# Search for the 512th score: one of three levels a round summed as signs on ScalarE, its row work cut into pieces between the rounds

## The reference, cut to what matters

```python
scores = xf @ gate_w.T
scores = (jnp.tanh(scores) + 1.0) * 0.5
vals, idx = jax.lax.top_k(scores.T, k)          # k = 4096 // 8 = 512, n = 8 experts
kept_w = vals.T
flat_idx = idx.T.reshape(-1)
y = xf[flat_idx].reshape(k, n, d)
y = _layernorm(y, ln_gamma, ln_beta)
h = jnp.einsum('knd,nfd->knf', y, fc1s) + b1s
h = jax.nn.gelu(h, approximate=True)
o = jnp.einsum('knf,ndf->knd', h, fc2s) + b2s
o = o * kept_w[:, :, None]
out = xf.at[flat_idx].add(o.reshape(k * n, d))
```

## Time and profile before

| | before |
|---|---|
| median of 3 runs | 853.91 us |
| lowest and highest | 852.01 and 854.15 us |
| the profiled execution's own time | 856.66 us |
| its span, from the first to the last instruction | 854.9 us |
| TensorE busy | 663.0 us, 78% of the span |
| VectorE busy | 555.0 us, 65% |
| ScalarE busy | 432.2 us, 51% |
| GpSimd busy | 405.3 us, 47% |
| mean granted TensorE clock | 0.896 of full speed |

### The profile page before, as it was taken

The page is one execution under the profiler, slowest core; times in us unless marked ns, Lnnn a source line. Parts: engine busy times, 40 slices in busy tenths (PEclk is TensorE's granted clock), DMA queues, the critical chain, the costliest instruction groups (busy, mean ns, idle before and its releaser), DMA issues. The chain is left out here.

```text
span 854.9 us, 18149 instructions
## 1 busy us (share of the span) xinstructions
PE 663.0 (78%) x6567; PEld 417.3 (49%) x6567; DVE 555.0 (65%) x1594; ACT 432.2 (51%) x627; POOL 405.3 (47%) x583
## 2 busy tenths in 40 slices
PE   6748999999869999999977669999896413888500
PEld 3423555555435666666644336766664103555400
DVE  6977888888468898888887643544456884222116
ACT  5433777777745555555526656766662600232102
POOL 7853777777640000000016756665564502788743
PEclk9975999999979999999989978999997755899765
DMA  4774463431000000000004999999991340355354
GB/s 159 244 221 94 135 169 97 120 95 54 4 1 1 1 1 2 1 1 1 2 0 177 264 257 174 189 178 173 187 183 55 91 114 17 74 129 98 34 94 124
DMA packets 134839, 85.76 MB, mean 100 GB/s; under 512 B 11104, under 2 KB 131424, under 8 KB 134624
## 3 DMA queue, kind: packets, MB, share of 16 engines
q1 hardware_dynamic: 127968, 79.30, 40.7%
q0 software_dynamic: 5632, 4.33, 3.7%
q10 hardware_dynamic: 1152, 0.98, 0.4%
HBM read 54.70 MB, written 29.49 MB: 98 GB/s over the span
## 5 line engine op out<-in xcount | busy, mean ns | idle before, releaser
L2120 ACT ACTIVATE a_prob<-a_ps_pair 128x1024 f32<-128x1024 f32 x96 | 93.8, 1023 | 51.9 <-PE a_ps_pair L1956 34.0
L1791 ACT ACTIVATE a_prob<-a_ps_pair 128x1024 f32<-128x1024 f32 x96 | 96.5, 1023 | 14.0 <-PE a_ps_pair L1594 10.9
L2132 POOL TENSOR_SCALAR_AFFINE_SELECT a_prob<-a_prob 128x512 f32<-128x512 f32 (+1 forms) x96 | 76.8, 805 | 55.0 <-ACT a_prob L2120 54.8
L1832 POOL TENSOR_SCALAR_AFFINE_SELECT a_prob<-a_prob 128x512 f32<-128x512 f32 (+1 forms) x96 | 75.4, 787 | 42.0 <-ACT a_prob L1791 41.3
L1730 DVE TENSOR_REDUCE a_mx<-a_ps_pair 128x4 f32<-128x1024 f32 x64 | 77.8, 1221 | 24.5 <-PE a_ps_pair L1635 22.8
L922 POOL TENSOR_SCALAR xn<-xn,stats,norm_b_rstd 128x128 f32<-128x128 f32 x8 | 6.4, 805 | 175.0 <-POOLq L411 175.0
L478 PEld LDWEIGHTS m_ps_n<-wd,m_act 128*128 128x128 f32 x512 | 66.4, 192 | 29.0 <-issue 27.4
L701 ACT ACTIVATE m_up<-m_ps_u,m_bup 128x512 f32<-128x512 f32 x64 | 44.0, 687 | 65.4 <-PE m_ps_u L466 65.3
L590 DVE SCALAR_TENSOR_TENSOR xn<-m_ps_n,m_wt,xn 128x128 f32<-128x128 f32 x256 | 71.7, 343 | 0.2 <-DVE xn L590 0.2
L478 PE MATMUL m_ps_n<-wd,m_act 128*128 128x128 f32 x512 | 67.6, 275 | 1.0 <-DVE xn L590 0.8
L466 PE MATMUL m_ps_u<-m_x1T,wgu 128*128 128x512 f32 x128 | 67.0, 606 | 0.0
(11 more groups left out here) (287 smaller groups left out, 1525.8 us busy)
## 6 DMA issues: line engine op xcount, KB each, us to landing
qst<-scratch_q SPq DMA_DIRECT2D x64, 128.0 KB, 4.2
kst<-scratch_k SPq DMA_DIRECT2D x64, 128.0 KB, 4.2
scratch_q<-p_parts SPq DMA_DIRECT2D x16, 384.0 KB, 3.1
scratch_k<-p_parts SPq DMA_DIRECT2D x16, 384.0 KB, 2.8
qst<-scratch_q SPq DMA_DIRECT2D x32, 192.0 KB, 6.1
kst<-scratch_k SPq DMA_DIRECT2D x32, 192.0 KB, 6.0
...
```

The costliest lines, as they stand in the source:

```text
L1791: nc.scalar.activation(prob[:, r % 6, :], pair[(0, 2, 1)[j]][:, :], ACT.Exp, scale=scale, bias=0.0).then_inc(s_e, 1)
L1832: nc.gpsimd.affine_select(out=blk, in_=blk, compare_op=ALU.is_ge, fill=0.0, base=0, pattern=[[0, n], [1, P]], channel_multiplier=-1).then_ ...
L2120: nc.scalar.activation(prob[:, r % 6, :], pair[r % 2][:, :], ACT.Square, scale=scale, bias=1.0).then_inc(s_e, 1)
L2132: nc.gpsimd.affine_select(out=blk, in_=blk, compare_op=ALU.is_ge, fill=0.0, base=0, pattern=[[0, n], [1, P]], channel_multiplier=-1).then_ ...
```

## The change

Rounds 1 to 12 still test three levels, but VectorE counts only two of them. The third is done by ScalarE: it computes the sign of score minus level for all 256 columns and writes the sum of the signs into the third column of `count`. The sum of signs over 4096 scores is twice the count minus 4096, so the third flag compares with 2*512 - 4096 - 0.5 (`sides`). ScalarE adds its bias, so the third level is kept with a negative sign, and the steps have signs too. TensorE waits for both engines' columns. Round 13 tests two levels on VectorE, with four small operations after it in place of two. ScalarE's other work in the block is spread over the rounds: two tiles of `yn` after the signs of each of rounds 1 to 8, and a quarter of `twice` (two instructions of four tiles) after those of rounds 9 to 12. `yn` is therefore complete before `twice`, and SP stores it first; the store of `twice` gets a semaphore of its own, which GpSimd waits for ahead of the first scatter and not ahead of the gathers. One more constant is loaded. The diff, whole:

```diff
--- before.py
+++ after.py
@@ -972,8 +972,8 @@
 
 
     ident, F = consts["ident"], F1
-    wgp, table, same, lower, slot, row, own, sel4, tilew, gb = [consts["later"][n] for n in (
-        "wgp", "table", "same", "lower", "slot", "row", "own", "sel4", "tilew", "gb1")]
+    wgp, table, sides, same, lower, slot, row, own, sel4, tilew, gb = [consts["later"][n] for n in (
+        "wgp", "table", "sides", "same", "lower", "slot", "row", "own", "sel4", "tilew", "gb1")]
     NT = NTILE
     sum_d = nc.dram_tensor("sum", [NTOK, C], F32, kind="Internal").ap()
     rows_d = nc.dram_tensor("normed", [NTOK, ROW], F32, kind="Internal").ap()
@@ -997,8 +997,9 @@
         yn = sb("yn", [P, NT, ROW])
         tanh = sb("tanh", [P, T])
         score = sb("score", [P, T])
-        hit = sb("hit", [P, 3, T], BF16)
-        count, parted = sb("count", [P, 3], BF16), sb("parted", [P, 2], BF16)
+        hit = sb("hit", [P, 2, T], BF16)
+        side = sb("side", [P, T], BF16)
+        count, parted = sb("count", [P, 4], BF16), sb("parted", [P, 2], BF16)
         level, base = sb("level", [P, 4]), sb("base", [P, 4])
         flag = sb("flag", [P, 3])
         reached, thr, need, before_sel = [sb(n, [P, 1]) for n in ("reached", "thr", "need", "before_sel")]
@@ -1048,8 +1049,11 @@
         s_ynp = sem("rows_normalised_by_pool")
         s_w = [sem(f"expert_weights_loaded{i}") for i in range(2)]
         s_d = sem("rows_stored")
+        s_sd = sem("sums_stored")
         s_st = sem("vector_step")
+        s_level = sem("levels_ready")
         s_cnt = sem("rows_counted")
+        s_side = sem("sides_summed")
         s_tot = sem("tokens_counted")
         s_part = sem("flags_counted")
         s_pre = sem("prefixes_ready")
@@ -1096,12 +1100,12 @@
             def _(sp):
                 for e in range(2):
                     sp.dma_start(w[:, e, :], io["w1"][e, :, :]).then_inc(s_w[e], 16)
-                sp.wait_ge(s_two, 1)
-                sp.dma_start(sum_d.rearrange("(t p) c -> p t c", p=P), twice[:, :, :]).then_inc(s_d, 16)
                 sp.wait_ge(s_yn, NT // 2)
                 sp.wait_ge(s_ynp, NT // 2)
                 sp.wait_ge(s_scol, 2)
                 sp.dma_start(rows_d.rearrange("(t p) c -> p t c", p=P), yn[:, :, :]).then_inc(s_d, 16)
+                sp.wait_ge(s_two, 8)
+                sp.dma_start(sum_d.rearrange("(t p) c -> p t c", p=P), twice[:, :, :]).then_inc(s_sd, 16)
                 for e in range(2, E):
                     sp.wait_ge(s_ob, e - 1)
                     sp.dma_start(w[:, e % 2, :], io["w1"][e, :, :]).then_inc(s_w[e % 2], 16)
@@ -1148,8 +1152,9 @@
                 last.then_inc(s_stp, 1)
 
                 for r in range(ROUNDS):
-                    n = 3 if r + 1 < ROUNDS else 1
-                    pe.wait_ge(s_cnt, 3 * r + n)
+                    n = 3 if r + 1 < ROUNDS else 2
+                    pe.wait_ge(s_cnt, 2 * r + 2)
+                    pe.wait_ge(s_side, min(r + 1, ROUNDS - 1))
                     nc.tensor.matmul(ps_c[:, 0:n], same[:, :].bitcast(BF16), count[:, 0:n], start=True, stop=True).then_inc(s_tot, 1)
 
                 pe.wait_ge(s_part, 2)
@@ -1225,8 +1230,7 @@
                     ins.then_inc(s_st, 1)
                     ve.wait_ge(s_st, done[0])
 
-                v.tensor_copy(level[:, :], table[:, 0:4]).then_inc(s_st, 1)
-                done[0] += 1
+                v.tensor_copy(level[:, :], table[:, 0:4]).then_inc(s_level, 1)
                 for c in range(NCH):
                     if c == 4:
                         norm.invert_rest(ve, s_rest)
@@ -1242,25 +1246,29 @@
                 v.tensor_scalar(score[:, :], tanh[:, :], 1.0, 0.5, ALU.add, ALU.mult).then_inc(s_score, 1)
                 ve.wait_ge(s_score, 1)
                 for r in range(ROUNDS):
-
-                    step_size = table[:, 4 * r:4 * r + 1]
-                    for j in range(3 if r + 1 < ROUNDS else 1):
+                    steps = table[:, 8 * r + 4:8 * r + 8]
+                    ve.wait_ge(s_level, r + 1)
+                    for j in range(2):
                         v.tensor_scalar(hit[:, j, :], score[:, :], level[:, j:j + 1], 0.0, ALU.is_ge, ALU.add,
                                         accum_out=count[:, j:j + 1]).then_inc(s_cnt, 1)
                     if r + 2 < ROUNDS:
-                        v.tensor_scalar(base[:, :], table[:, 4 * r + 4:4 * r + 8], level[:, 3:4], None, ALU.add).then_inc(s_st, 1)
+                        v.scalar_tensor_tensor(base[:, :], sides[:, 0:4], level[:, 3:4], table[:, 8 * r + 8:8 * r + 12], ALU.mult, ALU.add)\
+                            .then_inc(s_st, 1)
                         done[0] += 1
                     ve.wait_ge(s_tot, r + 1)
+                    if r + 1 < ROUNDS:
+                        step(v.scalar_tensor_tensor(flag[:, :], ps_c[:, 0:3], 0.0, sides[:, 4:7], ALU.add, ALU.is_ge, accum_out=reached[:, :]))
                     if r + 2 < ROUNDS:
-                        step(v.tensor_scalar(flag[:, :], ps_c[:, 0:3], CAP - 0.5, 0.0, ALU.is_ge, ALU.add, accum_out=reached[:, :]))
-                        step(v.scalar_tensor_tensor(level[:, :], step_size.to_broadcast([P, 4]), reached[:, 0:1], base[:, :], ALU.mult, ALU.add))
+                        v.scalar_tensor_tensor(level[:, :], steps, reached[:, 0:1], base[:, :], ALU.mult, ALU.add).then_inc(s_level, 1)
                     elif r + 2 == ROUNDS:
-                        step(v.tensor_scalar(flag[:, :], ps_c[:, 0:3], CAP - 0.5, 0.0, ALU.is_ge, ALU.add, accum_out=reached[:, :]))
-                        step(v.scalar_tensor_tensor(thr[:, :], step_size, reached[:, 0:1], level[:, 3:4], ALU.mult, ALU.add))
-                        step(v.tensor_scalar(level[:, 0:1], table[:, 4 * r + 4:4 * r + 5], thr[:, 0:1], None, ALU.add))
+                        step(v.scalar_tensor_tensor(thr[:, :], steps[:, 0:1], reached[:, 0:1], level[:, 3:4], ALU.mult, ALU.add))
+                        v.tensor_scalar(level[:, 0:2], table[:, 8 * r + 8:8 * r + 10], thr[:, 0:1], None, ALU.add).then_inc(s_level, 1)
                     else:
-                        step(v.tensor_scalar(reached[:, :], ps_c[:, 0:1], CAP - 0.5, None, ALU.is_ge))
-                        step(v.scalar_tensor_tensor(thr[:, :], step_size, reached[:, 0:1], thr[:, :], ALU.mult, ALU.add))
+                        step(v.tensor_scalar(flag[:, 0:2], ps_c[:, 0:2], CAP - 0.5, None, ALU.is_ge))
+                        v.scalar_tensor_tensor(thr[:, :], steps[:, 0:1], flag[:, 0:1], thr[:, :], ALU.mult, ALU.add).then_inc(s_st, 1)
+                        done[0] += 1
+                        step(v.tensor_tensor(level[:, 2:3], level[:, 1:2], flag[:, 1:2], ALU.mult))
+                        step(v.tensor_tensor(thr[:, :], thr[:, :], level[:, 2:3], ALU.max))
 
                 v.tensor_scalar(more[:, :], score[:, :], thr[:, 0:1], 0.0, ALU.is_gt, ALU.add, accum_out=parted[:, 0:1]).then_inc(s_part, 1)
                 v.tensor_scalar(equal[:, :], score[:, :], thr[:, 0:1], 0.0, ALU.is_equal, ALU.add, accum_out=parted[:, 1:2]).then_inc(s_part, 1)
@@ -1361,12 +1369,26 @@
                 for h in range(2):
                     nc.scalar.activation(yn[:, h:NT:2, C:ROW].rearrange("p (j g) e -> p g j e", g=4),
                                          ps_t[:, h * P:h * P + P].rearrange("p (g j e) -> p g j e", g=4, e=E), ACT.Copy).then_inc(s_scol, 1)
+                act.wait_ge(s_score, 1)
+
+                def sum_sides(r):
+                    act.wait_ge(s_level, r + 1)
+                    with nc.allow_low_precision("sums of signs are whole numbers up to 256"):
+                        nc.scalar.activation(side[:, :], score[:, :], ACT.Sign, bias=level[:, 2:3], accum_out=count[:, 2:3])\
+                            .then_inc(s_side, 1)
+
                 act.wait_ge(s_x3, 3 * NCH)
                 act.wait_ge(s_x3p, NCH)
-                nc.scalar.activation(twice[:, :, :], xn[:, :, :], ACT.Copy, scale=2.0).then_inc(s_two, 1)
-                act.wait_ge(s_yr, 12)
-                for t in range(0, NT, 2):
-                    nc.scalar.activation(yn[:, t, 0:C], xn[:, t, :], ACT.Copy, scale=yr[:, t:t + 1]).then_inc(s_yn, 1)
+                for r in range(ROUNDS - 1):
+                    sum_sides(r)
+                    if r == 0:
+                        act.wait_ge(s_yr, 12)
+                    if r < 8:
+                        for t in (4 * r, 4 * r + 2):
+                            nc.scalar.activation(yn[:, t, 0:C], xn[:, t, :], ACT.Copy, scale=yr[:, t:t + 1]).then_inc(s_yn, 1)
+                    else:
+                        for t in (8 * r - 64, 8 * r - 60):
+                            nc.scalar.activation(twice[:, t:t + 4, :], xn[:, t:t + 4, :], ACT.Copy, scale=2.0).then_inc(s_two, 1)
                 nc.scalar.activation(primer[:, :], yr[:, 0:1], ACT.Gelu_apprx_tanh)
                 for e in range(E):
                     after(act, s_o, e - 1)
@@ -1411,10 +1433,11 @@
```

(16 more changed lines are left out.)

## The result

Median of five runs 849.04 us (847.98 to 850.15) against 853.91 us (851.48 to 855.43, five runs): the ratio is 0.9948, 95% interval 0.9926 to 0.9970. The forecast was 850.5 us in 849.0 to 852.6. Two later comparisons of the same two kernels gave 0.9956 (0.9941 to 0.9972) and 0.9962 (0.9947 to 0.9978), so the gain is 3.2 to 4.4 us by the three ratios, and the middle of each is past 0.3%.

What follows compares the result with a forecast made beforehand. The serial chain of waits was taken as the bound, with VectorE's counting in the search on it. -4.43 + 0.18 + 0.70 + 0.1 = -3.45 us took the median from 853.91 to 850.5 us, range 849.0 to 852.6.

Steps and rivals of the forecast that it cites:

- Rounds 2 to 12: Search: VectorE's third count leaves eleven rounds, the signs hidden under two counts; 2.03 to 1.63 us each, -4.43 us.
- the pieces: ScalarE's row work between signs: hidden in rounds 1 to 8, large pieces in 9 to 12 perhaps late; +0.1 us, at most 0.7.
- Round 1: Search start: ScalarE makes two copies before its signs, so TensorE starts later; +0.18 us (0.09 to 0.21).
- Round 13: Search end: a second count on VectorE and four small operations for two; +0.70 us.
- Flags in the new form: Each search round: flags by `scalar_tensor_tensor` with accumulator instead of `tensor_scalar`; 0 taken, up to 0.7 us kept.
- The added wait: GpSimd's new wait before the first scatter, for a store landed long before; costs and brings nothing.
- The clock: TensorE's clock over one-hot products and expert 0 may rise at another point; 0 taken, -1 to +2 us kept.
- The rival of a later rise: Clock rises later in the one-hot products and expert 0; +2 us of the 3.45, 852.5 us; chance 0.09.
- the constant: One more load issue on SP's queue in layer 0's attention, taken up by its waiting; 0, at most 0.4 us.
- ScalarE late only in round 1: Rival: signs and read late in each of eleven rounds; gain only some 1.5 us, 852.4 us; chance 0.12.
- no table load: Rival: a 1.28 us table load before round 1's signs; gain falls to -2.2 us, 851.7 us; chance 0.06.
- the accumulator read: Rival: the read after each sum of signs drains ScalarE; at 0.7 us no shorter search, kernel possibly 856.1; chance 0.05.

Runs made afterwards that it cites:

- e2_signs_twice: Changed kernel with a second, unused instruction of the same signs ahead of each sum of signs; search 25.22 us, profiled execution 852.19 us.
- e3_pool_later: Changed kernel with GpSimd's tiles of the rows held back until the levels of round 6; search 22.88 us, profiled execution 851.49 us.
- e1_vector_counts_all: Changed kernel, but VectorE counts all three levels of rounds 1 to 12 and ScalarE sums no signs; ratio 1.0000 to the kernel before.

## Why the prediction was right, point by point

The sign, the size and the range were right, and the mechanism in the search was the one forecast. That the whole fits is in part luck: behind the flags 1.19 us were lost where the forecast took nothing, and 0.3 to 2.1 us, by the three ratios, were gained ahead of the search, where it took nothing too. The first comparison's 849.04 us is 0.04 us inside the range's lower end; in the two later ones the medians differ by 3.3 us (850.49 against 853.79, 849.90 against 853.21), next to the 3.4 forecast. The profiled execution, forecast at 853.2, took 849.08, mostly because the one before had waited in its attention. The terms:

- **Rounds 2 to 12**: -4.43 forecast, with +0.1 for the pieces. Measured 22.79 to 18.56 us, -4.23. The signs' path was as built: the instruction took 0.51 us against 0.474, its read 0.19 against 0.18, together 0.61 us because the read starts 0.1 us before the first one's end; 0.65 was taken. The Trainium skill, in "ScalarE: Activation LUTs", section "What ACT_TABLE_LOAD costs", gives about 280 ns and 0.833 ns an element for an instruction whose bias is a pointer; the estimate by it for 256 elements is 0.49 us. The trace has 0.507. The slack was forecast at 0.24 us, from a hand-over of 0.05 us; the hand-over measured 0.14 (`e2_signs_twice`), and with 0.61 the slack is 0.20. (The prediction's own "at about 0.68 us, plus some 0.05" leaves 0.21 under 0.94; its 0.24 goes with 0.65.)
- **What took most of 0.2 us off it** is a term I had left out: VectorE's small steps beside GpSimd's writes, 0.11 us in each of rounds 2 to 4 (`e3_pool_later`). Before, it showed in one round, of 2.21 us. So the sign "rounds 2 to 8 of 1.63 us" held for rounds 5 to 8 only.
- **Round 1**: +0.18 forecast, 2.05 to 2.24 us measured, +0.19.
- **Round 13**: +0.70 forecast, 1.22 to 1.88, +0.66.
- **The pieces**: +0.1 forecast, 0 measured. Rounds 9 to 11 are 1.63 or 1.64 us; two large pieces take 1.13 us together (bounds 0.9 to 1.3), and the signs of the next round start on time.
- **Flags in the new form**: 0 forecast, 0 measured (0.16 us both).
- **The search in all**: -3.45 forecast, -3.38 measured.
- **The added wait**: "cost and bring nothing". This step failed: +0.53 us. I had priced the wait by its semaphore, which was set long before, and not by its place, between GpSimd's last gather and a wait that is on the path. One of the prediction's signs of being wrong showed it: the first gather moved by 8.70 us (718.51 to 709.81) and the first scatter by 7.97 (740.23 to 732.26).
- **The clock**: 0 taken, -1 to +2 kept. From 17.3 to 18.1 us behind the flags it cost 0.39 us up to the index list and 0.20 in expert 0. With 0.53 that is 1.12 of the 1.19 us that the part behind the flags lost. The rival of a later rise, at 2 us and a chance of 0.09, came in at 0.6.
- **Stages ahead**: taken as unchanged. In the pair of profiles they differ by 5.71 us, most of it spread between executions. By the profiles the change itself is worth -3.38 + 0.53 and the clock's share, 2.3 to 2.9 us; the three comparisons have 3.2 to 4.4. The missing 0.3 to 2.1 us may come from ahead of the search, with the constant (0.9 us by its middle, its interval reaching past nothing; `e1_vector_counts_all` points the same way), and were not settled. The forecast put the constant at nothing or a loss of up to 0.4, never at a gain.
- **The rivals**: ScalarE late only in round 1, as forecast; no table load; the accumulator read is 0.19 us and not 0.7; the gathers did not wait for stores.
- **The range**: its slow end of -2.3 adds only one of the two terms of 0.7 us (the pieces, the flags' new form). With both it is -1.6, 852.3 us, still inside the range stated; neither term came.
